# One-pass key features, wider row and pick transfers, and a reordered adjacency stage in a four-layer graph network kernel

## The reference, cut to what matters

```python
# layer 0, mixing (Performer), for each of 2 depths and 8 heads
def softmax_kernel(data, proj, is_query, eps=0.0001):
    data_dash = einsum('bhnd,md->bhnm', data * normalizer, proj)      # 256 features
    diag = sum(data ** 2, -1) * 0.5 * normalizer ** 2
    m = max(data_dash, -1) if is_query else max(data_dash, (-2, -1))  # keys: one max a head
    return ratio * (exp(data_dash - diag - m) + eps)
ctx = einsum('bhnm,bhnd->bhmd', kp, v)     # kp: key features; v has a column of ones beside it

# layers 1 to 3, feed-forward: each token goes to 2 of 8 experts
out = sum(gates * expert_out[chosen], axis=1);  x = x + out;  xn = layernorm(x)

# layer 0, graph part
deg = segment_sum(1, row) ; norm = rsqrt(deg)[row] * rsqrt(deg)[col]
out = relu(segment_sum(norm * (xn @ W.T + b)[row], col))
```

## Time and profile before

| | |
|---|---|
| median of 3 runs | 3503.59 us (3499.82 to 3516.89) |
| the profiled execution's own time | 3513.79 us |
| its span | 3512.0 us |
| mean granted TensorE clock | 0.911 |
| PE busy | 3019.0 us, 86% |
| DVE busy | 1613.7 us, 46% |
| POOL busy | 1203.6 us, 34% |
| ACT busy | 986.2 us, 28% |

### The profile page before, as it was taken

The page is one execution under the profiler, slowest core; times in us unless marked ns, Lnnn a source line. Parts: engine busy times, 40 slices in busy tenths (PEclk is TensorE's granted clock), DMA queues, the critical chain, the costliest instruction groups (busy, mean ns, idle before and its releaser), DMA issues. The chain is left out here.

```text
span 3512.0 us, 45692 instructions
## 1 busy us (share of the span) xinstructions
PE 3019.0 (86%) x16957; PEld 1887.5 (54%) x16957; DVE 1613.7 (46%) x3263; ACT 986.2 (28%) x2302; POOL 1203.6 (34%) x1465
## 2 busy tenths in 40 slices
PE   7888999899899989979996955999599948589975
PEld 4543567655556756545544544777355635344553
DVE  8743334832442662467414553222425356542454
ACT  3212145432304542321203222444202215300132
POOL 3010566667365757832202221111203206400033
PEclk9988999999899989979997986999799959889888
DMA  2002243333033433341100003999501039700078
GB/s 63 4 15 78 87 156 120 123 102 115 33 123 117 158 106 108 120 116 37 36 1 24 25 25 143 417 417 414 174 0 37 19 118 320 233 12 0 30 286 288
DMA packets 171314, 421.44 MB, mean 120 GB/s; under 512 B 23576, under 2 KB 75320, under 8 KB 149863
## 3 DMA queue, kind: packets, MB, share of 16 engines
q1 hardware_dynamic: 153965, 368.22, 30.4%
q0 software_dynamic: 12960, 42.48, 3.1%
q10 hardware_dynamic: 4180, 7.95, 0.9%
HBM read 328.43 MB, written 90.15 MB: 119 GB/s over the span
## 5 line engine op out<-in xcount | busy, mean ns | idle before, releaser
L2159 POOL TENSOR_SCALAR raw<-raw 128x512 f32<-128x512 f32 x380 | 251.7, 662 | 1345.6 <-PE ps L402 670.4
L414 PE MATMUL ps<-units,ARENA 128*125 128x512 f16 x2880 | 636.3, 383 | 9.7 <-DVE ARENA L1452 5.3
L402 PE MATMUL ps<-ARENA,units 128*128 128x500 f16 (+1 forms) x2952 | 534.3, 343 | 6.7 <-ACT ARENA L1104 4.9
L414 PEld LDWEIGHTS ps<-units,ARENA 128*125 128x125 f16 x2880 | 391.1, 138 | 249.7 <-DVE X L1889 16.4
L402 PEld LDWEIGHTS ps<-ARENA,units 128*128 128x128 f16 x2952 | 288.9, 98 | 251.8 <-issue 17.0
L1440 DVE TENSOR_TENSOR ARENA<-tmp,ARENA 128x500 f16<-128x500 f32 (+3 forms) x289 | 196.7, 686 | 415.4 <-ACT ARENA L1104 233.1
L370 PE MATMUL ps<-ident,ARENA 125*128 125x125 f32 x560 | 116.7, 365 | 209.4 <-DVE ARENA L1428 93.5
L428 PE MATMUL ps<-ARENA,AT 125*125 125x512 f32 x600 | 260.2, 596 | 13.1 <-issue 12.3
L1103 ACT ACTIVATE tmp<-ps,cols 128x500 f32<-128x500 f32 (+1 forms) x204 | 131.2, 643 | 465.2 <-PE ps L402 453.9
L513 PE MATMUL ps<-proj,ARENA 128*125 128x512 f32 x480 | 248.8, 630 | 2.2 <-ACT ARENA L1201 1.1
L2163 POOL TENSOR_TENSOR AT<-raw,AT 128x512 f16<-128x512 f32 x200 | 236.5, 1183 | 17.0
(11 more groups left out here) (384 smaller groups left out, 4291.4 us busy)
## 6 DMA issues: line engine op xcount, KB each, us to landing
ARENA<-split_d SPq DMA_DIRECT2D x135, 1024.0 KB
raw<-in_moe SPq DMA_DIRECT2D x200, 256.0 KB, 2.9
split_d<-AT SPq DMA_DIRECT2D x200, 256.0 KB, 2.5
raw<-in_units SPq DMA_DIRECT2D x180, 256.0 KB, 2.5
ARENA<-split_d SPq DMA_DIRECT2D x27, 1280.0 KB
adj_d<-AT SPq DMA_DIRECT2D x1, 5468.8 KB
AT<-adj_d SPq DMA_DIRECT2D x1, 5468.8 KB
rows_d<-ARENA SPq DMA_DIRECT2D x6, 896.0 KB
```

The lines of the kernel that those rows point to most:

```text
L402: ins = pe.matmul(o[:, 0:nt * R], wt, mv_, start=(i == 0), stop=(i == len(steps) - 1))
L414: ins = pe.matmul(o[0:R, :], th(srcT, h, k, t, 1), w(k, g), start=(i == 0), stop=(i == len(steps) - 1))
L2159: pool.tensor_scalar(r, r, WEIGHT_SCALE, 1.0, ALU.mult, ALU.mult).then_inc(sem("pool_step"), 1)
```

## The change

1. **Keys in one pass.** Each product gets its exponential with the maximum of its own row; the difference to the head's maximum goes into the values as a factor (`v_scaled`), and the 1e-4 into a sum of the values that is added to `ctx` at the end (`v_eps`). `KP_LAG` is 14, and the features lie in 17 slots in AT's space, so ACT waits until AT is stored.
2. **Transfers.** Tokens in `rows_d` and `picks_d` are numbered p*10+t instead of t*125+p, so the tiles of a chunk lie side by side for a partition. The picks come in chunks of 2, 4 and 4 tiles.
3. **Merge.** POOL's sums are gone; DVE adds both picks. In layers 1 and 2 ACT writes the normalized tiles (`ln_scales`, `ln_root(M)`).
4. **SP's order.** `routed_experts` comes right after the quarters of its unit, ahead of the rows that are due.
5. **Adjacency stage.** POOL splits unit 1 only after `hs`; degrees of a tile are summed before its eviction; ACT takes a dummy root ahead; the gather waits for its tiles one by one.

```diff
-KP_LAG = 3
+KP_LAG = 14
+KP_SLOTS = 17
+PICK_CHUNKS = [(0, 2), (2, 4), (6, 4)]
-        kp_slot = [Q[0:R, i * D:(i + 1) * D] for i in range(4)]
+        kp_slot = [AT[0:R, 2048 + i * D:2048 + (i + 1) * D] for i in range(KP_SLOTS)]
...
 load_picks
-            for c, (t0, nt) in enumerate(CH):
+            for c, (t0, nt) in enumerate(PICK_CHUNKS):
...
-                                  picks_d[k * PICK + t0 * R:k * PICK + (t0 + nt) * R, :].rearrange("(t p) d -> p t d", p=R)[p0:p1])\
+                                  picks_d[k * PICK:k * PICK + N, :].rearrange("(p t) d -> p t d", t=T)[p0:p1, t0:t0 + nt, :])\
...
 gather_N, on PE
-                if src_name:
-                    pe.wait_ge(sem(src_name), s.more(src_name, T))
...
+                        if src_name and dt == 0:
+                            pe.wait_ge(sem(src_name), s.more(src_name, 1))
...
 keys, on PE: the first loop of 40 products and the one transpose and product of the maxima go
-                for t in range(T):
-                    for hp in range(4):
-                        pe.wait_ge(*left("dve"))
-                        head_pair(K, t, hp, bank("dve", "read_dve")).then_inc(sem("filled_dve"), 1)
...
+                    if T <= i < 5 * T and i % T == 1:
+                        pe.wait_ge(sem("kh"), s.more("kh", 1))
...
+                        pe.transpose(o[0:2, 0:R], kh[:, 2 * hp:2 * hp + 2], ident[0:R, 0:R]).then_inc(sem("filled_dve"), 1)
+                    if T <= i < 5 * T and i % T == 2:
+                        pe.wait_ge(sem("dg2"), s.more("dg2", 1))
...
+                        pe.matmul(o[0:R, 0:2], ones[0:2, 0:R], dg2, start=True, stop=True).then_inc(sem("filled_dve"), 1)
+                    if T <= i < 5 * T and i % T == 7:
+                        pe.wait_ge(sem("v_sum"), s.more("v_sum", 1))
...
+                        pe.matmul(o[:, 0:2 * DA], ones[0:R, :], v_sums[(i // T - 1) % 2], start=True, stop=True).then_inc(sem("filled_dve"), 1)
                     if i >= KP_LAG:
                         hp, t = divmod(i - KP_LAG, T)
                         if t == 0:
+                            pe.wait_ge(sem("v_scaled"), s.more("v_scaled", 1))
...
-                        pe.wait_ge(sem("kpe"), s.more("kpe", 1))
+                        pe.wait_ge(sem("kp"), s.more("kp", 1))
...
 keys, on ACT
+                act.wait_ge(sem("adj_stored"), 16 * len(PARTITION_CUTS))
...
+                        act.wait_ge(sem("kmax"), s.more("kmax", 1))
...
+                    if T <= i < 5 * T and i % T == 2:
+                        act.wait_ge(sem("key_gain_in"), s.more("key_gain_in", 1))
+                        act.activation(key_gain, key_gain, ACT.Exp).then_inc(sem("key_gain"), s.one("key_gain"))
...
 keys, on DVE, for each i below 40, and once in ten the rest
+                        dve.tensor_reduce(kmx[0:R, h:h + 2], o[0:R, :].rearrange("p (h m) -> p h m", h=2), AX_X, ALU.max).then_inc(sem("dve_step"), s.one("dve_step"))
+                        dve.wait_ge(*s.latest())
+                        stt(nb[0:R, h:h + 2], diag[0:R, h:h + 2], -1.0, kmx[0:R, h:h + 2], ALU.mult, ALU.subtract).then_inc(sem("kmax"), s.one("kmax"))
+                        if t == T - 1:
+                            dve.tensor_reduce(kh[:, 2 * hp:2 * hp + 2], kmx3[:, :, 2 * hp:2 * hp + 2].rearrange("p t h -> p h t"), AX_X, ALU.max).then_inc(sem("kh"), s.one("kh"))
...
+                        dve.tensor_reduce(km2, o[0:2, 0:R], AX_X, ALU.max).then_inc(sem("read_dve"), s.one("read_dve"))
+                        dve.wait_ge(*s.latest())
+                        ts(dg2, ident[0:2, 0:2], km2, None, ALU.mult).then_inc(sem("dg2"), s.one("dg2"))
...
+                        tt(key_gain, kmx3[:, :, heads], o[0:R, 0:2].unsqueeze(1).to_broadcast([R, T, 2]), ALU.subtract).then_inc(sem("key_gain_in"), s.one("key_gain_in"))
+                    if T <= i < 5 * T and i % T == 3:
+                        dve.wait_ge(sem("key_gain"), s.more("key_gain", 1))
+                        tt(v_scaled[(i // T - 1) % 2], vaug_all[:, :, heads, :], key_gain.unsqueeze(3).to_broadcast([R, T, 2, DA]), ALU.mult).then_inc(sem("v_scaled"), s.one("v_scaled"))
+                    if T <= i < 5 * T and i % T == 5:
+                        dve.tensor_reduce(v_sums[(i // T - 1) % 2].rearrange("p (h a) -> p h a", a=DA), vaug_all[:, :, heads, :].rearrange("p t h a -> p h a t"),
+                                          AX_X, ALU.add).then_inc(sem("v_sum"), s.one("v_sum"))
...
-                        ts(sl, sl, 1e-4, None, ALU.add).then_inc(sem("kpe"), s.one("kpe"))
...
+                        tt(ctxv[:, 2 * hp:2 * hp + 2, :, :], o[:, 0:4 * DA].rearrange("p (h m a) -> p h m a", h=2, a=DA),
+                           v_eps[:, 2 * hp:2 * hp + 2, :].unsqueeze(2).to_broadcast([128, 2, 2, DA]), ALU.add).then_inc(sem("ctx"), s.one("ctx"))
...
 merge, on DVE
+                for c, (t0, nt) in enumerate(PICK_CHUNKS):
+                    dve.wait_ge(sem(f"picks_back{c}"), 16 * 2 * len(PARTITION_CUTS) * layer)
+                    for t in range(t0, t0 + nt):
+                        tt(nat(X, t), nat(X, t), nat(back[0], t), ALU.add).then_inc(sem("dve_step"), s.one("dve_step"))
+                        dve.wait_ge(*s.latest())
+                        tt(nat(X, t), nat(X, t), nat(back[1], t), ALU.add).then_inc(sem(name), s.one(name))
...
-            add_picks(1, lambda t: ln_tile(X, M, "xn", t))
-            dve.wait_ge(*s.latest())
+            add_picks(1, lambda t: ln_scales(X, t))
...
 merge, on ACT (in ln_root)
+                    if normed is not None:
+                        act.wait_ge(sem("ln_scales"), s.more("ln_scales", 1))
+                        for t in range(t0, t0 + nt):
+                            act.activation(nat(normed, t), nat(X, t), ACT.Identity, bias=mv[0:R, t, 1:2], scale=rstd[0:R, t:t + 1]).then_inc(sem("normed"), s.one("normed"))
...
 adjacency stage, on ACT, DVE and POOL
+            act.activation(std[0:R, :], ones[0:R, 0:T], ACT.Sqrt)
             act.wait_ge(sem("degrees"), s.more("degrees", 1))
...
             for t in range(T):
+                dve.tensor_reduce(outdeg[0:R, t:t + 1], AT[0:R, t * N:(t + 1) * N], AX_X, ALU.add).then_inc(sem("dve_step"), s.one("dve_step"))
+                if t == T - 1:
+                    dve.wait_ge(*s.latest())
+                    then(dve.tensor_reduce(indeg[0:R, :], indeg3[0:R, :, :], AX_X, ALU.add))
+                    ts(outdeg[0:R, :], outdeg[0:R, :], 1.0, None, ALU.add).then_inc(sem("degrees"), s.one("degrees"))
...
                 stt(nat(Y, t), o[0:R, :], WS, b, ALU.mult, ALU.add).then_inc(sem("read_dve"), s.one("read_dve"))
-                dve.tensor_reduce(outdeg[0:R, t:t + 1], AT[0:R, t * N:(t + 1) * N], AX_X, ALU.add).then_inc(sem("dve_step"), s.one("dve_step"))
...
+                    if u == 1:
+                        pool.wait_ge(sem("hs"), T)
...
 SP: stores to rows_d, and the place of routed_experts in the loop over units
-                        sp.dma_start(rows_d[t0 * R:(t0 + nt) * R, :].rearrange("(t p) d -> p t d", p=R)[p0:p1],
+                        sp.dma_start(rows_d.rearrange("(p t) d -> p t d", t=T)[p0:p1, t0:t0 + nt, :],
...
                     quarter += 1
+                for layer in ROUTED_AFTER:
+                    if u == ROUTED_AFTER[layer]:
+                        while rows_sent <= ROWS.index(f"E{layer}"):
+                            load_row(rows_sent)
+                            rows_sent += 1
+                        routed_experts(layer)
                 while rows_sent < len(ROWS) and row_pos[rows_sent - ROW_SLOTS] + 1 <= u:
```

More of the change, by code:

```diff
@@ L158, in build @@
         EPS_LN, EPS_PHI, EPS_RMS = consts[:, 0:1], consts[:, 1:2], consts[:, 2:3]
-        kp_slot = [Q[0:R, i * D:(i + 1) * D] for i in range(4)]
+        kp_slot = [AT[0:R, 2048 + i * D:2048 + (i + 1) * D] for i in range(KP_SLOTS)]
+        v_scaled = [v.rearrange("p (t h a) -> p t h a", t=T, a=DA) for v in (Q[0:R, 0:T * 2 * DA], AT[0:R, 2048 + KP_SLOTS * D:2048 + KP_SLOTS * D + T * 2 * DA])]
+        v_sums = [tmp[0:R, i, 0:2 * DA] for i in range(2)]
+        v_eps = Q[:, 1300:1300 + HEADS * DA].rearrange("p (h a) -> p h a", a=DA)
+        vaug_all = Y[0:R, :].rearrange("p (t h a) -> p t h a", h=HEADS, a=DA)
+        key_gain = small[0:R, 32:32 + 2 * T].rearrange("p (t h) -> p t h", h=2)
         ctxv = Q[:, 4 * D:4 * D + HEADS * 2 * DA].rearrange("p (h m a) -> p h m a", m=2, a=DA)
@@ L1593, in _ @@
                 copy_diag()
-                for t in range(T):
-                    for hp in range(4):
+                s.seen["filled_act"] = marks[f"key_banks{dep}"]
+                kmx3 = kmx[0:R, :].rearrange("p (t h) -> p t h", h=8)
+                dve.wait_ge(*s.latest())
+                for i in range(4 * T + KP_LAG):
+                    heads = slice(2 * (i // T - 1), 2 * (i // T))
+                    if i < 4 * T:
+                        hp, t = divmod(i, T)
+                        h = t * 8 + 2 * hp
```

(44 more changed lines are left out.)

96 lines of the change are left out of this document (32 added, 64 removed).

## The result

| | before | after |
|---|---|---|
| median | 3510.24 us (4 runs, 3499.82 to 3519.12) | 3417.93 us (4 runs, 3413.69 to 3424.82) |
| ratio | | 0.974, 95% interval 0.9703 to 0.9777 |
| span of the profiled execution | 3512.0 us | 3423.1 us |
| mean granted TensorE clock | 0.911 | 0.913 |
| busy: PE, DVE, POOL, ACT | 3019.0, 1613.7, 1203.6, 986.2 us | 2969.2, 1606.2, 1169.7, 1005.0 us |

The forecast was 3390 us, with a range of 3362 to 3424. The time is inside, but 28 us above the forecast: of 113 us foreseen, the spans show 88.9. I read the two traces at the same places of the program.

What follows compares the result with a forecast made beforehand. PE was taken to bound the kernel, so edits pay by cutting its work or idle places. Terms 44+6.5+10.5+1.5+35+11+4.5 = 113 us, against the median of 3503.6, gave 3390 us, range 3362 to 3424.

Steps and rivals of the forecast that it cites:

- Keys in one pass, 44 us forecast: Key stages of two depths: 91.0 us each instead of 112.9, 22 saved a depth, range 14 to 28.
- The steps up to the first `ctx` part: Key stage's front: 16.1 us for 14 products alone, 3 for filling and table load, 4.2 for maxima, gain and `v_scaled`.
- the last 14 `ctx` parts at 0.90 = 12.6: End of each key stage: 14 `ctx` parts left after the pairs, 0.90 us each, 12.6 us in all.
- DVE and POOL bind (rival): Key stage: DVE's added work beside busy POOL loses 9 to 17 us a depth, total 3414 us; chance 0.12.
- Adjacency stage, 6.5+10.5+1.5: Adjacency stage: 6.5 us from unit 1's late split, 10.5 from an earlier gather start, 1.5 from keeping the high clock.
- SP's order, 35 us: Routing of layers 1 and 2: SP no longer waits for a row before storing `rows_d`; 17.5 us each, range 28 to 36.5.
- Transfers and merge, 15.5 us: Merges: faster pick loads and a smaller first chunk save 5.5 us each in layers 1 and 2, 4.5 in layer 3.
- The change makes runs of 4 and 8 KB: Pick loads: 2 KB runs move at 269 GB/s, 8 KB weight runs at 415; longer runs should exceed 350.
- The third rival: Merges: picks come no faster, by a rule asking 1 MiB a transfer; merges give 0 to 3 us, 3404 us; chance 0.10.
- the rivals on DVE and on the routing: DVE: 3414 us, chance 0.12. Routing: gathers stay late behind weight loads or another wait, 3420 us, chance 0.05.

Runs made afterwards that it cites:

- c3: The kernel before with one line of the change, POOL splitting the second unit only after the rows are scaled; 3501.63 us, ratio 0.9974.
- b3: The changed kernel with both picks loaded from SP's queue, chunk by chunk, and none from ACT's; 3420.74 us, ratio 0.9752.

## Why the prediction was nearly right, and where it failed

- **Keys in one pass, 44 us forecast:** 36.4 in the changed trace (33.2 with the projections behind them), 37 alone. The steps up to the first `ctx` part held: 23.1 against 23.3 us, the maximum at 0.69, `v_scaled` at 1.5. The term that was mis-sized is "the last 14 `ctx` parts at 0.90 = 12.6": seven of them ran at 1.72 and three at about 1.65, since the clock fell. With the three small products among them the 14 parts took about 21 us in the changed trace. At the full clock the stage takes 87, 4 less than the 91 forecast: a pair takes 1.75 us where 1.82 was taken, 1.7 in all, and waits and small products came out some 2 us shorter. So part of the loss in the tail was made up by luck elsewhere. I took 0.90 from a stretch where wide products stood beside the narrow ones, and did not ask what clock narrow ones get alone.
- **DVE and POOL bind (rival):** no. The offset took 0.342 us in the mean, against 0.42 taken.
- **Adjacency stage, 6.5+10.5+1.5:** 5.1+11.5+2.1, right in sum. What I had missed is that the late split also frees the scalings, which I had priced at 0.76 in either case: c3 shows 7.0 us by the last degree sum (6.5 forecast) and 3.7 behind it. In the changed kernel most of those 3.7 should be hidden by the reordering too, so they did not change the sum. The 1.5 us for the clock behind a short wait came as 2.1.
- **SP's order, 35 us:** 34.6 in the traces and 35 alone.
- **Transfers and merge, 15.5 us:** 1.1. The failed step is "The change makes runs of 4 and 8 KB", taken to bring the loads to the 415 GB/s of the weights. The slow and the fast loads of the earlier trace rows differ in the length of the runs and also in the partitions (125 cut at 112, against 128), which stands in the kernel, and I priced the first. The third rival had the right outcome, by a rule about size that the runs do not bear out. It was priced at 14 us, which is what was lost.
- **The range** held because it took in the rivals and 10 us for how executions scatter. Its upper end was set by the rivals on DVE and on the routing, and neither came true. What came, the third rival and a loss in the keys together, was no case of its own, so that their sum stayed inside is in part luck. The two losses, 7.6 (10.8 with the projections) and 14.4, make 22 to 25 of the 28 us; up to 6.6 more is how far the medians of before lie apart (3503.6 when the forecast was made, 3510.2 now).

## What to carry to other kernels

When a slow transfer and a fast one differ in more than one thing, list all of them (run length, partitions, queue, source) before pricing one; here loads of 125 partitions, cut at 112, moved 243 to 276 GB/s where 128 in one transfer moved 421 to 425, so a few unused partitions can be cheaper than an exact shape. A loop that is taken apart leaves a tail of its cheapest products: do not price it at what they cost beside wide ones, and read its granted clock over several executions. Wide products beside such a tail are worth a trial; here they went with the full clock, but a gain in time was not shown. Where two engines share work, look at which of a line's effects lie elsewhere: one wait on POOL sped up DVE at two places.

## What the runs showed of the hardware that I had not expected

- Loads of 125 partitions cut at 112 moved 243 to 276 GB/s with the DMA engines full, in 2 KB, 4 KB and 8 KB runs, on one queue or two; 128 partitions in one transfer, in 4 and 8 KB runs, 421 to 425.
- PE can be busy all the time and still get the low clock. In b3's second depth the middle of the key stage stayed there for 44 us and the stage took 113.7; one stretch of it:

```profile
975.00:1000.00 25.00, 24.93 (x75) 17.44 (x76) 10.45 (x19) 5.88 (x14) 18.95 (x24) 0.50 0.56 165
```

PE was busy 24.93 of 25 us at 0.50. The same pairs of one wide and one narrow product ran at 1.00 in all the other stages but for 10 us or less. What keeps them at the low level once they are there is open.
